# Causal attention in slots of four heads: maxima from row scores, exponentials from column scores, weighing on four array column strips

## The chip, the core and the metric

The kernel runs on one core of a Trainium2 chip, as one launch that computes everything. The metric is device microseconds from start to end; lower is better. TensorE (PE in the rows, PEld for its weight loads) multiplies matrices into the eight banks of PSUM; VectorE (DVE), ScalarE (ACT) and GpSimd (POOL) work elementwise; SyncE (SP) issues the DMAs. Each engine follows its own list of instructions in order, and they meet only through semaphores.

## The reference

The input is x of 8 sequences, 512 tokens, 128 channels. The output is x plus two branches of its layer-normalised tokens xn: a causal attention, which the change is about, and a stack of six layers of windowed attention and gated MLP, which it leaves alone.

```python
q_lat = (x @ Wq_down).reshape(b, t, H, L)             # H 16 heads, L 64; k and v alike
q_c, q_e = q_lat @ Wq_up_c, q_lat @ Wq_up_e           # 4 + 4 dimensions a head
q = concatenate([q_c, rope(q_e)]);  k alike;  v = v_lat @ Wv_up    # 8 dimensions a head
scores = einsum('bhqd,bhkd->bhqk', q, k) / sqrt(8)
scores = where(causal, scores, -inf)
att = softmax(scores, axis=-1)
y = einsum('bhqk,bhkd->bhqd', att, v)
return y @ Wc                                         # 128 x 128
```

Per sequence there are 16 heads of 512 x 512 scores under a causal mask, with only 8 dimensions to contract.

## The kernel before, in words

**Start.** The tokens of all 8 sequences are normalised and turned into `xT` (channels on partitions). The down and up weights are multiplied into five 128 x 128 matrices `wcomb`. This ends at about 36 us.

**The causal stage** runs over the batches b (sequences) and, in a batch, over 64 slots n, one for each head h and query tile qt of 128 queries. The helper `causal` (L254) runs a function `causal_slot` on each engine over the first batch, a hardware loop over the middle ones and the last batch with its drain; `earlier` (L263) gives the slot that lies a fixed lag behind. Within one turn of the slot the engines do, for different lags:

- GpSimd, `mask_q` (L1267): once a head it multiplies a stack of q by a 0/1 mask, so that of the four heads in a stack only one is left. The stack holds for four heads the terms hi·hi, hi·lo, lo·hi of q and k as rows (`stacks`, 128 rows), filled by SP with small transfers of 64 KB (`stack`, L292).
- TensorE (L402): the scores of 128 queries by (qt+1) x 128 keys as one fp32r product over all 128 rows into one of three banks, then the triangle `tri` added to the diagonal block by a bf16 product with the identity. The query rows lie on partitions. Seven slots later it transposes the divided exponentials, 128 x 128 blocks in fp32 (L416). Fifteen slots later it weighs the values: `v16` holds each head's values in 128 columns that are zero elsewhere, so that all heads add up into one bank `ps[4]` over the batch.
- VectorE (L997): the negated row maximum (L1013) and, five slots later, the division of the exponentials (L1009).
- ScalarE (L708): the exponential with the maximum as bias and the row sum as second output (L722), and the copy of the transposes to SBUF (L668, a helper that records every copy).

In the same lists stand the five projections of the next batch (`project_causal`, L384), their rotation and split into hi and lo on VectorE (`rope`, L972), the product with `wc` and the sum with x (L1019). Before the projections VectorE copies the batch's part of `xT` to `xb` (L970).

**After it** the weights of the first of six layers are loaded, once the last weighing product is done, and the rest of the kernel follows. L357 is the line of the helper that records every matrix product, so such rows are told apart by their tiles: `sb_xwin,sb_ptT` are the causal scores, `sb_tri,sb_identb` their masks, plain `sb_area` 128x512 and narrower the weighing. An fp32 product appears as two records, an fp32r or bf16 product as one; a transpose in fp32 is one.

In the windowed attention, unchanged, two kinds of products use halves of the array: scores with 64 stationary columns (`128*64 128x64`), whose two results go to partitions 0 to 63 and 64 to 127, and weighings with 64 rows (`64*128 64x256`), whose operands lie on partitions 0 to 63 and 64 to 127.

## Time and profile before

| | |
|---|---|
| time, median of 3 runs | 4157.45 us (4157.35 to 4159.3) |
| profiled execution: time, span | 4155.5 us, 4153.7 us |
| busy share TensorE, VectorE, ScalarE, GpSimd | 92%, 78%, 75%, 60% |
| mean granted TensorE clock | 0.971 |
| first causal score, last weighing product | 60.75 us, 709.9 us |
| DMA moved | 52.9 MB, 13 GB/s |

The span is the time from the first to the last instruction. Busy shares are means over the whole kernel; the causal stage is the first sixth of it. A row of the timeline gives the start, how long the group was busy, the engine, the line, the operation, the result and operands, the shape of weights and moving data, and the count; square brackets give idle time before it. Matrix products are pipelined: one product's time includes about 0.16 us in which the next already runs. The granted clock is a share of 2.4 GHz.

### The profile page before, as it was taken

The page shows a single profiled execution, that of the slowest core. Times are in us where ns is not written, and L with a number is a line of the kernel's source. Part 1 is how long each engine was busy: PE and PEld are TensorE (multiplying, and loading weights), DVE is VectorE, ACT ScalarE, POOL GpSimd, SP SyncE. Part 2 cuts the span into 40 slices and gives each one's busy share as a digit, 9 for nine tenths or more (in the row PEclk, how much of TensorE's full clock was granted, in tenths as well). Part 3 has the DMA queues.
Part 4 walks back from the last instruction along what each step waited for, and adds up shares of the span by engine and source line. Part 5 has one row for each costly group of instructions (what it writes and reads, how often), then busy time and mean ns, then how long its engine had stood idle before and what let it go on. Part 6 is the DMA issues. An engine that isn't in the chain of part 4 may idle for free.

```text
span 4153.7 us, 101302 instructions
## 1 busy us (share of the span) xinstructions
PE 3814.5 (92%) x30950; PEld 2939.8 (71%) x31328; DVE 3258.6 (78%) x5635; ACT 3109.2 (75%) x7150; POOL 2498.3 (60%) x2247
## 2 busy tenths in 40 slices
PE   6999998899998999988999989999889999899998
PEld 4666665677766777766777667777667776677776
DVE  5877876888867888768888678887688886788876
ACT  4777776788866888857888668887578886688875
POOL 1221221777745777737777457776377774577763
PEclk9999999999998999998999989999989999999999
DMA  2111111000010000010000100000100000000002
GB/s 79 42 32 31 29 39 35 2 0 0 0 28 1 1 0 0 1 28 1 0 0 0 28 1 1 0 0 1 28 1 0 0 0 28 1 1 0 0 1 68
DMA packets 53261, 52.86 MB, mean 13 GB/s; under 512 B 13574, under 2 KB 40452, under 8 KB 51972
## 3 DMA queue, kind: packets, MB, share of 16 engines
q1 hardware_dynamic: 52996, 49.77, 4.5%
q8 instruction: 113, 1.85, 0.2%
q14 instruction: 152, 1.25, 0.1%
HBM read 28.77 MB, written 4.19 MB: 8 GB/s over the span
## 4 chain that ended last, share of the span: by engine, by line
issue 26%; PE 24%; ACT 24%; DVE 21%; ACTq 2%; DVEq 2%; POOL 1%; SPq 0%; DMA 0%; POOLq 0%
PE bank L357 19%; ACT sb_area L668 12%; DVE sb_ssq L1105 10%; DVE sb_smax L1116 6%; ACT sb_area L777 5%; PE bank L416 3%; ACT sb_lnb L786 3%; ACT sb_lnb L789 3%; DVE sb_area L1093 1%; PE bank L503 1%; POOL sb_area L1336 1%; DVE sb_nmx L1013 1%; DVE sb_area L1119 0%; PE bank L532 0%; DVE sb_area L1009 0%
## 5 line engine op out<-in xcount | busy, mean ns | idle before, releaser
L668 ACT ACTIVATE sb_area<-bank 128x512 f32<-128x512 f32 (+4 forms) x3029 | 1570.3, 553 | 259.0 <-PE bank L357 182.3
L357 PE MATMUL bank<-sb_area 128*64 128x64 f32 (+4 forms) x16624 | 1286.1, 274 | 94.9 <-issue 57.8
L1093 DVE TENSOR_TENSOR sb_area<-bank,sb_rots 128x1024 f32<-128x1024 f32 x768 | 939.2, 1224 | 395.2 <-ACT sb_area L777 394.4
L1311 POOL TENSOR_TENSOR sb_area<-sb_area,sb_rn 128x512 f32<-128x512 f32 x768 | 784.8, 1043 | 608.5 <-ACT sb_rn L793 608.5
L1297 POOL TENSOR_TENSOR sb_area<-sb_area 128x512 f32<-128x512 f32 x768 | 967.9, 1278 | 78.3 <-DVE sb_area L1093 76.2
L357 PEld LDWEIGHTS bank<-sb_area 128*64 128x64 f32 (+2 forms) x16624 | 849.5, 151 | 200.6 <-issue 139.1
L357 PE MATMUL bank<-sb_wqk_hi,sb_xwin 128*128 128x512 f32 x1536 | 729.7, 477 | 53.9 <-DVE sb_xwin L1073 43.6
L357 PE MATMUL bank<-sb_area,sb_wvo 128*128 128x256 f32 x3072 | 728.3, 381 | 3.1 <-DVE sb_xT L1151 3.1
L357 PEld LDWEIGHTS bank<-sb_area,sb_wvo 128*128 128x128 f32 x3072 | 555.0, 190 | 78.3 <-issue 12.8
L503 PE MATMUL bank<-sb_ident,sb_area 128*128 128x128 f32 x3072 | 494.9, 285 | 33.4 <-ACT sb_area L668 31.0
L503 PEld LDWEIGHTS bank<-sb_ident,sb_area 128*128 128x128 f32 x3072 | 358.8, 144 | 227.6 <-issue 160.0
L1105 DVE TENSOR_REDUCE sb_ssq<-sb_area 128x8 f32<-128x512 f32 x768 | 486.7, 675 | 0.0
L777 ACT ACTIVATE sb_area<-bank 128x512 f32<-128x512 f32 x768 | 460.4, 600 | 30.9 <-PE bank L357 14.5
L1320 POOL TENSOR_TENSOR sb_area<-sb_area,sb_srec 128x512 f32<-128x512 f32 x384 | 400.3, 1042 | 88.4 <-DVE sb_srec L1131 88.4
L1270 POOL TENSOR_TENSOR sb_ptT<-sb_xwin,sb_hm 128x512 fp32r<-128x512 f32 x128 | 137.8, 1077 | 510.8 <-PE bank L357 494.1
L722 ACT ACTIVATE sb_area<-bank,sb_nmx 128x128 f32<-128x128 f32 (+3 forms) x512 | 270.1, 528 | 178.5 <-DVE sb_nmx L1013 175.6
L357 PEld LDWEIGHTS bank<-sb_wqk_hi,sb_xwin 128*128 128x128 f32 x1536 | 304.2, 198 | 111.3 <-issue 48.9
L1013 DVE TENSOR_REDUCE sb_nmx<-bank 128x1 f32<-128x128 f32 (+3 forms) x512 | 249.1, 487 | 125.4 <-PE bank L357 114.4
L357 PE MATMUL bank<-sb_wqk_lo,sb_xwin 128*128 128x512 f32 x768 | 315.4, 411 | 0.0
L820 ACT ACTIVATE sb_area<-sb_area 128x512 f32<-128x512 f32 x384 | 242.9, 633 | 76.4 <-DVE sb_area L1119 70.9
L357 PE MATMUL bank<-sb_xwin,sb_ptT 128*128 128x128 f32 (+3 forms) x512 | 286.9, 561 | 13.3 <-POOL sb_ptT L1270 8.4
L1129 DVE TENSOR_REDUCE sb_ssum<-sb_area 128x8 f32<-128x512 f32 x384 | 261.6, 681 | 45.2 <-ACT sb_area L820 40.0
(103 smaller groups left out, 4861.7 us busy)
## 6 DMA issues: line engine op xcount, KB each, us to landing
sb_xwin<-sb_p SPq DMA_DIRECT2D x256, 64.0 KB, 2.0
sb_area<-in_Wqkv SPq DMA_DIRECT2D x7, 1024.0 KB, 5.8
sb_area<-in_WvT SPq DMA_DIRECT2D x7, 512.0 KB, 7.3
sb_wo_bd<-in_Wo SPq DMA_DIRECT2D x14, 256.0 KB, 8.2
sb_area<-in_x SPq DMA_DIRECT2D x4, 512.0 KB, 5.7
sb_area<-in_x SPq DMA_DIRECT2D x8, 256.0 KB, 2.9
x_plus_causal<-sb_area SPq DMA_DIRECT2D x8, 256.0 KB, 2.3
out<-sb_area SPq DMA_DIRECT2D x8, 256.0 KB, 3.5
```

The source lines that it names most:

```text
L357: return nc.tensor.matmul(o, a, b, start=start, stop=stop, skip_group_check=True)
L503: m = nc.tensor.transpose(rbank[:, j * P:(j + 1) * P], qn[:, c, j * P:(j + 1) * P], ident[:, :])
L668: return nc.scalar.activation(o, i, ACT.Copy)
L722: nc.scalar.activation(ea(k // TT, qt, 0, (qt + 1) * P), ps[k % 3][:, 0:(qt + 1) * P], ACT.Exp, bias=nmx[:, k % 8:k % 8 + 1], accum_out=ls ...
L777: nc.scalar.activation(sqb[:, c % 2, :], pj[c % 2][:, :], ACT.Square).then_inc(S["sq"], 1)
L1013: nc.vector.tensor_reduce(nmx[:, k % 8:k % 8 + 1], ps[k % 3][:, 0:(k % TT + 1) * P], AX.X, ALU.max, negate=True).then_inc(S["c_max"], 1)
L1093: tt_(t12[:, c % 2, :, :].rearrange("p u (h d) -> p u h d", h=8), src, bc(rots[:, tt, s, :, :], [P, 2, 8, D], 2), ALU.mult).then_inc(S["ro ...
L1105: nc.vector.tensor_reduce(ssq[:, tt % 2, half, 8 * (c % 2):8 * (c % 2) + 8], sqb[:, c % 2, :].rearrange("p (h d) -> p h d", h=8), AX.X, AL ...
L1129: nc.vector.tensor_reduce(ssum[:, wp, :], d3, AX.X, ALU.add).then_inc(S["ssum"], 1)
L1297: pt_(qsum[:, c % 2, :].rearrange("p (h e d) -> p h e d", h=8, e=2), t12[:, c % 2, 0, :].rearrange("p (h e d) -> p h e d", h=8, e=2), swap ...
L1311: pt_(qn[:, c, :].rearrange("p (h d) -> p h d", h=8), qsum[:, c % 2, :].rearrange("p (h d) -> p h d", h=8), r, ALU.mult).then_inc(S["qn"], 1)
L1320: pt_(dd[:, wp, :].rearrange("p (h k) -> p h k", h=HP), dd[:, wp, :].rearrange("p (h k) -> p h k", h=HP), srec[:, wp, :].unsqueeze(2).to_b ...
```

## The change

The causal stage is rewritten; the rest stays. A slot is now a group of four heads of one batch, 32 slots in all, and all lists are written out over an iteration `it` from -2 to 7 and a head group `hg` of 0 to 3, without hardware loops.

- **Projections** of batch it+2 read `xT` itself and all go through bank 7, whose users take turns by one list (`m_order`, semaphore `m_free`): maxima, projections, values, output.
- **Stacks** hold each head on 32 partitions: 8 dimensions times four rows: three terms, and a fourth row that is 1 for k in two of the dimensions. q and k go to DRAM (`split_out`, six transfers of 256 KB) and come back in this order (`stack`, two transfers of 256 KB for each head group). Two batches are held.
- **Row scores** (`rows_of_scores`) for slot n1 = 4 it + 4 + hg serve only for the maxima: in eight units two heads at a time, each with 32 rows of the array, into banks 0 and 1, with the mask. VectorE takes both heads' maxima in one reduction (`maxima`). The maxima of a slot are turned once (`turn_max`), split in hi and lo, sent through DRAM and put into two of the stack's fourth rows of q (`max_rows`).
- **Column scores** (`columns_of_scores`) for slot n2 = 4 it + hg, four slots later: twelve tiles with the keys on partitions, 32 rows of the array each, in banks 2 to 4, with the mask. The product subtracts the maximum through the extra rows. ScalarE takes the exponential without bias or sum (`exp_columns`). No transposes.
- **Weighing** (`weigh_values`): four heads, each with 32 stationary columns, go to partitions 32r to 32r+31 of bank 5, and once more with `ones32` instead of the values for the sums, into bank 6. At a batch's end ScalarE takes exp(-ln(sum)), VectorE multiplies (`weighed_causal`, `divided`).
- GpSimd no longer masks anything.

```diff
+            def rows_of_scores(n, u):
+                a, hg, qt = n // 4, n % 4, u % 4
+                need(pe, "c_max", 8 * n + u)
+                if u == 0:
+                    pe.wait_ge(S[f"stack{hg}"], FULL * (a + 1))
+                keys = (qt + 1) * P
+                for x in range(2):
+                    r = 2 * (u // 4) + x
+                    rows = slice(32 * r, 32 * r + 32)
+                    mm(ps[x][:, 0:keys], stack_q[a % 2][rows, hg, qt * P:(qt + 1) * P], stack_k[a % 2][rows, hg, 0:keys],
+                       True, False)
+                for x in range(2):
+                    m = mm(ps[x][:, qt * P:keys], identb[:, :], tri[:, :], False, True)
+                m.then_inc(S["c_s1"], 1)
+
+            def columns_of_scores(n, j):
+                a, hg, r = n // 4, n % 4, j % 4
+                need(pe, "c_exp", 12 * n + j - 2)
+                if j == 0:
+                    pe.wait_ge(S[f"mrow{hg}"], 2 * 16 * (a + 1))
+                rows = slice(32 * r, 32 * r + 32)
+                o, k, q = ps[2 + j % 3], stack_k[a % 2][rows, hg, :], stack_q[a % 2][rows, hg, :]
+                for kt, c0 in (((0, 0),), ((1, 0),), ((2, 0), (3, 2 * P)))[j // 4]:
+                    mm(o[:, c0:c0 + T - kt * P], k[:, kt * P:(kt + 1) * P], q[:, kt * P:T], c0 == 0, False)
+                for c0 in (0, 2 * P)[0:1 + j // 8]:
+                    m = mm(o[:, c0:c0 + P], tri[:, :], identb[:, :], False, True)
+                m.then_inc(S["c_s2"], 1)
+
+            def weigh_values(n, kt, o, weights, last):
+                a, hg = n // 4, n % 4
+                e, c0 = ((et0, 0), (et1, 0), (et2, 0), (et2, 2 * P))[kt]
+                for r in range(4):
+                    m = mm(o[32 * r:32 * r + 32, kt * P:T], weights(kt, r), e[:, r, c0:c0 + T - kt * P],
+                           hg == 0 and kt == 0, hg == 3 and kt == 3)
+                if last:
+                    m.then_inc(S["c_pv"], 1)
...
+            for it in range(-2, B):
+                for hg in range(4):
+                    n2, n1 = 4 * it + hg, 4 * it + 4 + hg
...
+                    tiles(0, 1, 2)
+                    if n2 >= 1:
+                        end_of_slot(n2 - 1)
+                    if 0 <= n1 - 1 < SLOTS:
+                        turn_max(n1 - 1)
+                    unit(0)
+                    tiles(3)
+                    unit(1)
+                    tiles(4, 5)
+                    if hg < 2 and it + 2 < B:
+                        project_causal(it + 2, 2 * hg)
+                    if hg == 2 and it >= 1:
+                        causal_out(it - 1)
+                    unit(2)
+                    if n2 >= 0:
+                        weigh_causal(n2, 0)
+                    tiles(6)
+                    unit(3)
+                    if n2 >= 0:
+                        sum_causal(n2, 0, True)
+                    tiles(7, 8)
+                    if hg < 2 and it + 2 < B:
+                        project_causal(it + 2, 2 * hg + 1)
+                    if hg == 2 and 0 <= it + 1 < B:
+                        causal_values(it + 1)
+                    unit(4)
+                    if n2 >= 0:
+                        weigh_causal(n2, 1)
+                        sum_causal(n2, 1, True)
+                    tiles(9)
+                    unit(5)
+                    tiles(10)
+                    unit(6)
+                    tiles(11)
+                    unit(7)
+            end_of_slot(SLOTS - 1)
+            causal_out(B - 1)
...
+            def exp_columns(n, j):
+                T_, r = j // 4, j % 4
+                act.wait_ge(S["c_s2"], 12 * n + j + 1)
+                need(act, "c_pv", 3 * (n - 1) + T_ + 1)
+                w = T if T_ == 0 else T - P
+                nc.scalar.activation((et0, et1, et2)[T_][:, r, :], ps[2 + j % 3][:, 0:w], ACT.Exp).then_inc(S["c_exp"], 1)
...
+            def maxima(n, u):
+                r, qt = 2 * (u // 4), u % 4
+                dve.wait_ge(S["c_s1"], 8 * n + u + 1)
+                if u == 0 and n >= 2:
+                    dve.wait_ge(S["c_mt"], n - 1)
+                nc.vector.tensor_reduce(nmx[:, n % 2, 0:16].rearrange("p (r t) -> p r t", t=TT)[:, r:r + 2, qt],
+                                        banks[:, 0:2, 0:(qt + 1) * P], AX.X, ALU.max, negate=True).then_inc(S["c_max"], 1)
```

`end_of_slot` weighs and sums key tiles 2 and 3; `weigh_causal(n, kt)` and `sum_causal(n, kt)` call `weigh_values` with the values and with the ones; `tiles` and `unit` call the column and row scores where their slot exists.

## Rows read from the trace of the kernel before

**Rows 1.** The page, part 1: busy us (share of the span) and instructions of each engine.
```profile
PE 3814.5 (92%) x30950; PEld 2939.8 (71%) x31328; DVE 3258.6 (78%) x5635; ACT 3109.2 (75%) x7150; POOL 2498.3 (60%) x2247
```

**Rows 2.** Busy time by stretches: stretch, length, engines, granted clock, DMA share, GB/s; three batches.
```profile
138.00:219.00 81.00, 75.50 (x441) 50.75 (x440) 63.22 (x155) 59.50 (x193) 17.33 (x16) 0.98 0.13 34
...
300.00:382.30 82.30, 75.95 (x441) 51.07 (x441) 63.51 (x156) 59.77 (x194) 17.33 (x16) 0.98 0.13 33
...
628.00:710.00 82.00, 78.52 (x473) 54.08 (x473) 59.13 (x150) 62.76 (x202) 14.55 (x14) 1.00 0.05 13
```

**Rows 3.** Timeline of TensorE in the causal stage: start, us, engine, line, tiles, shapes, count.
```profile
694.09 0.48 PE L357 MATMUL bank<-sb_xwin,sb_ptT 128*128 128x512 f32 x1
...
697.69 0.61 PE L416 MATMUL bank<-sb_ident,sb_area 128*128 128x128 f32 x4
698.14 0.39 PE L357 MATMUL bank<-sb_area 128*128 128x128 f32 x2
698.28 0.48 PE L357 MATMUL bank<-sb_xwin,sb_ptT 128*128 128x512 f32 x1
698.60 0.23 PE L357 MATMUL bank<-sb_tri,sb_identb 128*128 128x128 bf16 x1
698.67 0.28 PE L416 MATMUL bank<-sb_ident,sb_area 128*128 128x128 f32 x1
698.79 1.02 PE L357 MATMUL bank<-sb_area 128*128 128x512 f32 x2
```

**Rows 4.** Timeline of TensorE in the windowed attention: full-array, column-half and row-half groups.
```profile
1004.22 1.89 PE L357 MATMUL bank<-sb_area,sb_wvo 128*128 128x256 f32 x8
...
1008.54 1.15 PE L357 MATMUL bank<-sb_area 128*64 128x64 f32 x32 [0.16 <-issue]
1009.62 0.44 PE L561 MATMUL bank<-sb_ident,sb_xs 128*128 128x128 f32 x2
1009.99 1.13 PE L357 MATMUL bank<-sb_area 64*128 64x256 f32 x8
1011.05 0.66 PE L503 MATMUL bank<-sb_ident,sb_area 128*128 128x128 f32 x4
```

**Rows 5.** Timeline of TensorE's weight loads there, with idle time before.
```profile
1009.99 0.73 PEld L357 LDWEIGHTS bank<-sb_area 64*128 64x128 f32 x8 [0.17 <-issue]
1011.05 0.42 PEld L503 LDWEIGHTS bank<-sb_ident,sb_area 128*128 128x128 f32 x4 [0.33 <-issue]
```

**Rows 6.** VectorE's reductions, six batches grouped by form (busy us, mean ns), and a start-up one.
```profile
L1013 DVE TENSOR_REDUCE sb_nmx<-bank 128x1 f32<-128x512 f32 x94 | 64.7, 689 | 12.7 <-PE bank L357 7.8
...
L1013 DVE TENSOR_REDUCE sb_nmx<-bank 128x1 f32<-128x256 f32 x95 | 40.1, 422 | 24.0 <-PE bank L357 24.0
...
4.52 1.22 DVE L957 TENSOR_REDUCE sb_lnm<-sb_area 128x8 f32<-128x1024 f32 x1 [0.75 <-DMA sb_area<-in_x]
```

**Rows 7.** ScalarE's exponentials of the causal stage by form, six batches.
```profile
L722 ACT ACTIVATE sb_area<-bank,sb_nmx 128x512 f32<-128x512 f32 x94 | 64.7, 689 | 32.8 <-DVE sb_nmx L1013 32.8
...
L722 ACT ACTIVATE sb_area<-bank,sb_nmx 128x384 f32<-128x384 f32 x94 | 54.6, 580 | 26.5 <-DVE sb_nmx L1013 25.8
```

**Rows 8.** Timeline before the first score.
```profile
35.52 7.65 DVE L970 COPY sb_area<-sb_xT 128x512 f32<-128x512 f32 x1 [9.39 <-ACT sb_xT L668]
...
43.31 3.75 PE L357 MATMUL bank<-sb_area 128*128 128x512 f32 x4 [8.46 <-DVE sb_area L970]
...
60.75 0.48 PE L357 MATMUL bank<-sb_xwin,sb_ptT 128*128 128x128 f32 x1 [8.43 <-POOL sb_ptT L1270]
```

**Rows 9.** TensorE by stretches: busy us, granted clock, DMA share, GB/s.
```profile
153.00:156.50 3.50, 1.10 (x10) 0.99 0.01 2
156.50:160.00 3.50, 3.45 (x9) 0.52 0.00 0
...
1308.00:1313.00 5.00, 1.89 (x8) 0.50 0.00 0
```

**Rows 10.** Timeline at the stage's end: last weighing products, and what waited for them.
```profile
705.17 4.70 PE L357 MATMUL bank<-sb_area 128*128 128x128 f32 x18
...
709.90 0.34 SPq L323 DMA_DIRECT2D sb_area<-in_Wqkv x1
...
719.42 2.19 ACT L668 ACTIVATE sb_wqk_hi<-sb_area 128x512 fp32r<-128x512 f32 x4 [8.91 <-DMA sb_qks<-in_qks]
```

398 lines of the change are left out of this document (208 added, 190 removed).

## The prediction

> **What bounds the kernel now.** I read the page's busy shares first [rows 1]: TensorE is the busiest engine, but that is a mean over stages. The table by stretches of time, cut at the batches of the causal attention, comes next [rows 2]. The stage runs from the first score at 60.75 us [rows 8] to the last weighing product at 709.9 us [rows 10], 649 us. In a batch of 81 to 82 us TensorE is busy 75 us, VectorE 63, ScalarE 60, GpSimd 17. TensorE bounds the stage, so a change gains what it takes off TensorE's stream of instructions and loses what it puts there. All that follows the stage has the same code and starts when the last weighing product is done; only the stage's end moves it.
>
> One head costs 4.19 us in the calm part of a batch (first score of one head at 694.09, of the next at 698.28). The timeline of such a head [rows 3] gives the prices at 2.4 GHz. An fp32 product is two records; the pair of 512 columns takes 1.02 us and one record 0.59, so a record of 512 columns costs 0.43 in the stream, of 128 columns 0.107. fp32r (scores) and bf16 (mask) columns cost half: 512 columns 0.213, 128 columns 0.053. A head has 1280 columns of scores (0.53), 512 of mask (0.21), ten transposes (1.07) and 1280 columns weighed in two records each (2.13), 3.95 us, with 0.04 for each mask's weights 4.1. Sixteen heads and 5.1 us of projections, values and output are 71 us; the other 10 to 11 us of a batch are waits around the projections.
>
> **Removed and added on TensorE.** I count by slot, the new unit: four heads, 32 slots; today one costs 20.4 us. Transposes (4.3 us) go. Weighing (8.5 us) becomes 16 products with 32 stationary columns each, on four column strips, and as many again for the sums. One after the other this would be 17.1 us, four abreast 4.27 us. Scores are computed twice: 5120 columns with 32 rows each for the maxima, and 5120 again as columns; masks 16 and 16.
>
> Do strips run abreast? [Rows 4] show halves. 32 records of 64 columns on two column halves take 1.15 us; one after the other they would be 32 x 0.053 + 0.17 = 1.9. Eight records of 256 columns on two row halves take 1.13; eight full-array ones take 1.89. So halves run in pairs, although each product is two records. Four abreast isn't shown. The ends are 4.27 us (four) and 8.5 us (two) a slot; I take four, since nothing in the pairs shows a shared limit. The Trainium skill, "TensorE: Matmul & The Clock Gate", Part 3, gives 2.38x for three column strips. If four strips were 3.2x by that, an estimate from that page, they would be 5.3 us and the kernel some 33 us longer than with my value; no run here shows it.
>
> What does changing the shape cost? In [rows 4] two full-array transposes start at 1009.62 and take 0.44, so the last starts 0.27 before their end, at 1009.79, and has its columns through at 1009.90. The row halves start at 1009.99: 0.09 later. Their group takes 1.13 where 4 x 0.216 + 0.16 = 1.02 is the columns and the tail: another 0.10, the first weights, which are not hidden. The loads agree: idle 0.17 before the halves and 0.33 before the return [rows 5], while in [rows 3] full-array groups follow each other without it. So a change of shape costs 0.09 plus the load: 0.107 for 128 fp32r columns, 0.03 for a 32-column strip, about 0.013 for bf16. The Trainium skill, "TensorEngine Tiling (Array Packing)", Key Properties, says that changing the mode, not just the tile, drains the engine, and lists 32-row tiles as a mode of their own; by it 32-row tiles pay what halves pay here, which the trace shows for halves alone.
>
> The new order changes shape all the time, since every 32-row score is followed by a full-array mask:
> - a tile of 512 columns: 0.20 + 0.213 + 0.10 + 0.053 = 0.57 us; 384 columns 0.52; 256+128 columns with two masks 0.59. Twelve tiles: 6.7 us.
> - a unit of row scores, two heads abreast, q+1 blocks of keys: 0.43 + 0.053(q+1). Eight units: 4.5 us.
> - weighing and sums: 4.27 + four changes at 0.12 + small gaps: 4.9 us; the turn of the maxima 0.1.
>
> 16.2 us a slot, some 6 of it shape changes. The bounds of a change of shape are 0 and 0.3 us (half clock); there are about 44 in a slot, so an error of 0.02 in each is 26 us of kernel time.
>
> **Waits added.** The row scores use one pair of banks, so unit u+1 is queued behind the reduction of unit u, and all of TensorE's later work behind it. VectorE takes 0.42, 0.69, about 0.96 and 1.22 us for 256 to 1024 columns ([rows 6], 1.06 ns a column, and 1.22 for 1024). Add 0.21 from the last mask column to its start and 0.06 back. A reduction of 1.22 us needs 1.5 us of other work behind its unit. Walking the written order, this holds for the first five units. Units 6 and 7 have only one tile each in between (0.52 to 0.59 us): 0.4 and 0.65 us of wait. A slot is 17.2 us. ScalarE's twelve exponentials are below 4 x 0.69 + 8 x 0.58 = 7.4 us [rows 7], the eight reductions 6.6: neither engine is near. In three slots of four two projections (0.85 each), or output and values, add 1.75: 18.95. A batch is 3 x 18.95 + 17.2 = 74, taken as 75 for small gaps that my count of a head misses too (4.1 against 4.19). GpSimd's masking and SP's 32 small transfers a batch are replaced by 8 transfers of 256 KB, 6 through DRAM before them, and the maxima's 3 per slot; these have one to four slots of lead, and I cost them at nothing. The cover for the maxima is three slots, 50 us, against four transfers of 2 to 3 us.
>
> **The pipeline's ends.** Today batches overlap without a seam. The new order has one pass of row scores only, seven with both, one of columns only.
> - First score: today 60.75 [rows 8]. The 7.65 us copy goes (7 us earlier), but one bank serves both projections (+2), and q and k go 1.5 MB out to DRAM and 0.5 back, about 12 us: 62 (56 to 68).
> - Row scores only: each unit is a bare chain of reduction and 0.61 + 0.053(q+1). A slot is 6.6 + 4.9 + 1.1 + 0.25 = 12.8; four are 51. TensorE is mostly idle there, as it was from 1308 to 1313 us (busy 1.89 of 5 us), where its clock was granted 0.50 [rows 9], the 1.2 GHz level. That adds up to 15; I take 8: 59.
> - Seven batches at 75: 525.
> - Columns only: 4 x 11.8 + 0.9 = 48. Last sums, behind the last exponential: 2.3.
>
> End at 62 + 59 + 525 + 48 + 2.3 = 696, against 709.9: 14 us earlier. The longer end (logarithm, exponential, product: +2.4 us) lies beside the weight load of 709.90 to 719.4 [rows 10] and costs nothing. With the clock held, the kernel takes 4157.45 - 14 = 4144.
>
> **The clock.** From 153 to 156.5 us TensorE is busy 1.10 of 3.5 us, and from 156.5 to 160 it is granted 0.52, although busy 3.45 [rows 9]. In the new slot the last tiles and units (about 13 to 17 us) stream for 1.1 of 3.4 us: the rest is changes of shape and waits on VectorE. I expect the lower level to come there in nearly every other slot and to last through the next slot's first tiles and sums, which take some 3 us more at half rate. That is 1.1 us a slot over 28: +31. Bounds: 0, and the whole stage at 1.2 GHz, where a slot is 27 to 32 us.
>
> **Forecast.** 4157.45 - 14 + 31 = 4175, say 4176. The profiled execution has a span of 4153.7 in a time of 4155.5, 2 us below the median, so differences carry over as they are.
>
> **Rivals.**
> 1. *The clock holds.* 4144 (4125 to 4160). For: a busy share over half in a slot as a whole. Against: [rows 9].
> 2. *Changing shape to 32-row tiles is cheaper than to halves.* Up to 44 x 0.09 = 4 us a slot, also no dip: 4060 to 4125. Against: the constant 0.09 in [rows 4, 5] both ways.
> 3. *Strips run only in pairs.* +4.27 x 32 = 137: 4280 to 4320. It would show as eight strip records taking four times one's stream time instead of twice.
> 4. *The clock stays low* (slower, and by much). A 32-row product may keep a quarter of the array at work; then the tiles and units of a slot hardly count as work and the level returns only sometimes. A slot at 26 to 27 us instead of 18.7: +230 to +250, 4380 to 4420. It decides once the granted clock of the seven full batches is under about 0.8.
> 5. *The extra work isn't the bound at all*, VectorE or DMA is: the first unit of each batch would wait on its stack. Each us there is 8 us; little speaks for it.
>
> **Chances.** Forecast (4150 to 4215) 0.35; clock holds 0.25; cheap changes 0.12; pairs only 0.08; clock low 0.17; the rest 0.03. A measurement of this kernel tells 0.2%, 8 us, from no change. Faster (under 4149): cheap changes 0.12 and most of clock holds 0.18, together 0.30. Same: 0.12. Slower: 0.58. The range takes in half of the cheap changes and half of the low clock: 4085 to 4410. The likeliest case alone is 4150 to 4215.
>
> **What would show it.** The score of a 32-row tile and its mask starting 0.09 after the columns of the one before are through; eight strip records of 512 columns in about 1.0 us; a full slot of 17 to 19 us at a clock of 1.00, with waits before units 6 and 7; the granted clock by stretches of 17 us between 60 and 700 us; first unit at 62 and last sum near 727. A slot under 15 us or over 24 at full clock would mean that my prices of the shapes are wrong.

## The result, and the profile after

The changed kernel takes 4292.9 us (median of 4 runs, 4288.9 to 4295.4) against 4157.4 us: 1.0324 times the time before, 95% interval 1.0306 to 1.0342. It is slower by 135 us, where 19 were forecast. The profiled execution has a span of 4287.1 us against 4153.7.

First the page of the changed kernel: span, busy shares, and the granted clock in 40 slices of 107 us.

```profile
span 4287.1 us, 98195 instructions
PE 4006.0 (93%) x32128; PEld 2850.4 (66%) x32128; DVE 3016.4 (70%) x4772; ACT 2853.0 (67%) x6048; POOL 2357.7 (55%) x2124
PEclk9878886699999899999999999999999999999999
```

TensorE is busier than in [rows 1], 4006 us against 3814, although it has hardly more products; VectorE, ScalarE and GpSimd all have less work than before. The clock row says where: it is below 9 in slices 2 to 8, which with the first are the causal stage, and like before behind it.

The first slice needs care, because there the granted clock and the durations disagree:

```profile
60.00:77.00 17.00, 11.66 (x39) 1.00 0.22 79
61.98 2.02 PE L382 MATMUL bank<-sb_xT,sb_area 128*128 128x512 f32 x2
```

The record says 1.00 from the first score to 149.5 us, but an fp32 product of 512 columns takes 2.02 us, where it takes 1.02 at 2.4 GHz in [rows 3], and such double durations last until about 146 us. In that stretch I go by the durations: the level was 1.2 GHz. From 150 us on the two agree in every row shown here.

The stage's two ends, from the timeline. The first row score starts at 59.96 us; SP's load for the layers, which waits for the last weighing product, is issued at 842.74, where it was at 709.90 in [rows 10].

```profile
59.96 0.47 PE L382 MATMUL bank<-sb_xwin 32*128 32x128 f32 x2 [12.59 <-DMA sb_xwin<-qk_rows]
842.74 0.35 SPq L348 DMA_DIRECT2D sb_area<-in_Wqkv  x1
```

842.74 - 709.90 = 132.8, and the spans differ by 133.4. So all of the loss lies in the stage. By stretches (us from the start, length, TensorE's busy time, granted clock, DMA share, GB/s), with the last row for the pass of column scores alone:

```profile
124.00:300.00 176.00, 171.35 (x952) 0.77 0.13 41
300.00:500.00 200.00, 194.04 (x1192) 0.79 0.16 50
500.00:700.00 200.00, 194.59 (x1198) 0.78 0.15 47
776.00:843.00 67.00, 64.80 (x425) 0.73 0.03 9
```

TensorE has work 97% of the time at a clock of 0.77 to 0.79 (the first row is too high by what was just said: with 22 us more at 1.2 GHz it is about 0.71); the three batches of [rows 2] were at 0.98 to 1.00. One calm batch slot by slot (a slot begins here with its first column mask), and a slot of the last full batch, which has no projections:

```profile
407.72:430.74 23.02, 22.36 (x135) 0.80 0.07 25
430.74:452.05 21.31, 20.65 (x134) 0.87 0.01 3
452.05:472.69 20.64, 19.98 (x147) 0.92 0.40 129
472.69:496.50 23.81, 23.15 (x131) 0.67 0.16 47
699.67:727.30 27.63, 27.52 (x130) 0.50 0.01 2
```

The same instructions take 21.3 us at 0.87 and 23.0 at 0.80. The slot at 0.50 takes 27.6 without projections, where the fourth, of the same form, takes 23.8 at 0.67. So the durations follow the clock. Read in steps of 0.1 us, the batch from 412.5 to 501.3 us has six dips to 0.50, together 34 us of 89: around 417.5, 433, 455, 475.5, 486 and 498 us. One long stretch at the full level and the longest dip:

```profile
437.00:453.00 16.00, 15.34 (x94) 1.00 0.01 2
480.50:490.50 10.00, 10.00 (x49) 0.51 0.36 107
```

The waits are small, 0.20 and 0.47 us before two of the eight units of a slot:

```profile
449.27 0.44 PE L382 MATMUL bank<-sb_xwin 32*128 32x384 f32 x2 [0.20 <-DVE sb_area L1115]
450.97 0.50 PE L382 MATMUL bank<-sb_xwin 32*128 32x512 f32 x2 [0.47 <-DVE sb_area L1115]
```

Where the clock is at 2.4 GHz the prices are the forecast ones. From the timeline of TensorE (`sb_xwin 32*128` and `sb_wqk_lo,sb_wqk_hi` are scores, `128*32` weighing on four strips):

```profile
541.54 0.50 PE L382 MATMUL bank<-sb_xwin 32*128 32x512 f32 x1
541.98 0.23 PE L382 MATMUL bank<-sb_identb,sb_tri 128*128 128x128 bf16 x1
542.13 2.79 PE L382 MATMUL bank<-sb_area 128*32 128x256 f32 x32
...
546.39 0.39 PE L382 MATMUL bank<-sb_wqk_lo,sb_wqk_hi 32*128 32x256 f32 x2
546.71 0.29 PE L382 MATMUL bank<-sb_tri,sb_identb 128*128 128x128 bf16 x2
546.92 0.44 PE L382 MATMUL bank<-sb_xwin 32*128 32x384 f32 x1
...
549.52 1.06 PE L382 MATMUL bank<-sb_area 128*32 128x512 f32 x8
550.51 0.44 PE L382 MATMUL bank<-sb_xwin 32*128 32x384 f32 x1
...
841.17 1.51 PE L382 MATMUL bank<-sb_area 128*32 128x256 f32 x32 [0.58 <-ACT sb_area L818]
```

A tile of 512 columns with its mask takes 542.13 - 541.54 = 0.59 us (forecast 0.57), a unit over two blocks of keys 546.92 - 546.39 = 0.53 (0.54), the eight strip records of 512 columns 550.51 - 549.52 = 0.99 ("about 1.0"). The 32 strip records that start at 542.13 already ran in a dip: 2.79 us, against 1.51 for the same at 841.17.

Setting each product of a dip to its time at 1.00 gives an estimate of the slots at full clock: 19.0 and 19.1 us for the slots at 430.74 and 452.05 (forecast 18.95), 17.2 for the one at 472.69 (forecast 17.2).

By passes, beside the forecast: row scores alone 63.4 us (59), seven full batches 123.77 to 776.17 = 652.4 (525, and 31 for the clock), columns alone with the last sums 66.6 (50), the start 1.6 us earlier than said (60.36, counted like the slots from the first mask; the first score itself is at 59.96). The question is therefore why the granted clock stays at three quarters in the full batches (0.76 by the record for all seven, 0.74 with the first stretch put right), and whether it alone is the loss.

### The profile page after: what moved, and what is told of

It is laid out like the page before. It is cut to its first block, busy times and chain, and to the rows that moved or that the text cites. A ratio compares the mean times of both kernels' runs of the same rounds, so it can differ in the third digit from the quotient of the medians.

```text
span 4287.1 us, 98195 instructions
## 1 busy us (share of the span) xinstructions
PE 4006.0 (93%) x32128; PEld 2850.4 (66%) x32128; DVE 3016.4 (70%) x4772; ACT 2853.0 (67%) x6048; POOL 2357.7 (55%) x2124
## 4 chain that ended last, share of the span: by engine, by line
PE 29%; issue 24%; ACT 22%; DVE 20%; ACTq 1%; DVEq 1%; POOL 1%; DMA 1%; SPq 0%; POOLq 0%
PE bank L382 27%; ACT sb_area L769 11%; DVE sb_ssq L1227 10%; DVE sb_smax L1238 5%; ACT sb_area L894 5%; ACT sb_lnb L903 3%; ACT sb_lnb L906 3%; DVE sb_area L1115 2%; PE bank L604 1%; DVE sb_area L1215 1%; POOL sb_area L1446 1%; DVE sb_area L1241 0%; PE bank L633 0%; ACT sb_rn L910 0%; ACTq L892 0%
## 5 line engine op out<-in xcount | busy, mean ns | idle before, releaser
L769 ACT ACTIVATE sb_area<-bank 128x512 f32<-128x512 f32 (+3 forms) x2517 | 1352.6, 578 | 251.8 <-PE bank L382 188.7
L382 PE MATMUL bank<-sb_area 128*64 128x64 f32 (+6 forms) x17520 | 1132.2, 304 | 7.4 <-DMA sb_area<-in_c_crot 2.8
L382 PEld LDWEIGHTS bank<-sb_area 128*64 128x64 f32 (+3 forms) x17520 | 743.7, 148 | 226.0 <-issue 177.3
L382 PEld LDWEIGHTS bank<-sb_area,sb_wvo 128*128 128x128 f32 x3072 | 555.0, 190 | 78.4 <-issue 12.8
L1115 DVE TENSOR_REDUCE sb_area<-bank 128x2 f32<-128x256 f32 (+3 forms) x256 | 211.5, 826 | 464.3 <-PE bank L382 464.1
L894 ACT ACTIVATE sb_area<-bank 128x512 f32<-128x512 f32 x768 | 460.6, 601 | 30.9 <-PE bank L382 13.9
L818 ACT ACTIVATE sb_area<-bank 128x384 f32<-128x384 f32 (+1 forms) x384 | 199.3, 523 | 416.6 <-PE bank L382 412.8
L1241 DVE TENSOR_TENSOR sb_area<-bank,sb_smax 128x512 f32<-128x512 f32 x384 | 265.6, 692 | 13.3
```

Of the source, the lines that this page charges most:

```text
L382: return nc.tensor.matmul(o, a, b, start=start, stop=stop, skip_group_check=True)
L769: return nc.scalar.activation(o, i, ACT.Copy)
L894: nc.scalar.activation(sqb[:, c % 2, :], pj[c % 2][:, :], ACT.Square).then_inc(S["sq"], 1)
L1115: nc.vector.tensor_reduce(nmx[:, n % 2, 0:16].rearrange("p (r t) -> p r t", t=TT)[:, r:r + 2, qt], banks[:, 0:2, 0:(qt + 1) * P], AX.X, AL ...
L1241: tt_(dd[:, wp, :].rearrange("p (h k) -> p h k", h=HP), s3, bc(smax[:, wp, :], [P, HP, 64], 2), ALU.subtract).then_inc(S["sub"], 1)
```

## The experiments

The theory on record with the runs: TensorE's stream has the length I worked out, and what is missing is the clock, lowered because products of 32 rows use little of the array or because changes of shape leave gaps. The rivals: the prices of that stream at full clock, or the waits, are wrong. Each kernel ran beside the kernel before on its chip (4154.5 to 4157.7 us).

### More columns in each tile: on the full array, or on 32 rows

```diff
+                mm(o, identb[:, :], lmask[:, 0, :], True, True)     # e1_fill_full
+                mm(o, k[:, 0:P], q[:, 0:T], True, True)             # e1_fill_rows
                 for kt, c0 in (((0, 0),), ((1, 0),), ((2, 0), (3, 2 * P)))[j // 4]:
```

> Work is added to the changed kernel (4292.9 us): ahead of the first score product of each of the 384 column tiles stands one more bf16 product over the whole array, 512 columns into the same bank, which the score product then overwrites. 0.213 us each at 2.4 GHz, 2.6 us a slot. Theory (the excess over my sum is TensorE's clock, which falls to 1.2 GHz where the array is lightly used): the level holds at 2.4 GHz in the full batches, where a slot takes about 21.2 us instead of the 23.3 of the changed kernel; in all about 4230 us, faster with more work. Rival (the slot is as long as it is for other reasons, waits or shape changes that I priced too low): the added work adds 12 x 0.23 us a slot, about 88 us: 4380.

Measured: 4386.3 us (4372.5 to 4400.1), ratio 1.0553 [1.0474, 1.0631]. That is the number of the rival without the clock, 4380. A slot of it without projections, at full clock, and 200 us in the middle:

```profile
793.69:813.33 19.64, 19.39 (x143) 1.00 0.01 3
300.00:500.00 200.00, 198.25 (x1115) 0.77 0.14 44
```

> The same added work in the stream, but with 32 rows of the array: ahead of the first score product of each column tile one more fp32r product of 512 columns on the same 32 rows, overwritten by the real one. 0.213 us each at 2.4 GHz as in the twin with full-array products. Theory (a 32-row product leaves most of the array idle and does not keep the clock up): the granted clock stays as low as in the changed kernel or lower, and the added work costs its columns at a mixed clock, 3 to 3.5 us a slot: about 4400. Rival (any stream of products keeps the clock up): the same as the twin, 4230. Rival without the clock: 4380, with an unchanged granted clock.

Measured: 4490.5 and 4571.6 us, too far apart for a ratio with an interval; the mean clock over the whole kernel was 0.905 and 0.882, in the twin 0.926 and 0.920. The profile is of the longer execution, its full slots 30.2 to 34.3 us long. The same 200 us of it:

```profile
300.00:500.00 200.00, 199.36 (x889) 0.55 0.13 40
```

The slot at 1.00 is worth most: 19.64 us, less 12 products at 0.213 (2.56), is 17.1 us, and the forecast for this slot was 17.2. Against the rival (waits or changes of shape priced too low) it is this slot that speaks, not the time. The size of the first result is a miss: twelve more full-array products in a slot did not lift the clock (0.71 to 0.84 from 124 to 900 us), they cost their own time and some more. But the two kernels have as many columns and as many changes of shape, and differ by 90 us at the least (4490.5 against 4400.1): in the profiled executions 512 columns more on 32 rows brought the level down to 0.55, the same columns on 128 rows left it at 0.77. The added products also differ in type, fp32r and bf16; the trains below are all of bf16.

### Column scores over all 128 rows

```diff
-                o, k, q = ps[2 + j % 3], stack_k[a % 2][rows, hg, :], stack_q[a % 2][rows, hg, :]
+                o, k, q = ps[2 + j % 3], stack_k[a % 2][:, hg, :], stack_q[a % 2][:, hg, :]
```

> The column scores are taken over all 128 rows of the stacks instead of the 32 rows of one head, so that a tile holds the sum over four heads of score minus maximum (the output is not the reference's). Same columns, same masks, no change of the array's shape inside a tile. By my prices a tile falls from 0.57, 0.52, 0.59 us to about 0.31, 0.26, 0.31: 3.2 us less a slot at a full clock, less about 1 us of new waits on the maxima. Theory with the clock: the level rises too, a slot goes from 23.3 to about 17 us, columns-only slots from 16 to 9: about 4090 (4070 to 4140). Rival without the clock: 32 x 3.2 = 100 us less, 4190.

Measured: 4110.1 us (4109.8 to 4110.3), ratio 0.9888 [0.9859, 0.9917]. The separation of the heads is left out: each column score sums the four heads of a stack.

```profile
300.00:500.00 200.00, 185.07 (x1525) 0.95 0.21 66
```

The time lies in the range of the theory with the clock (4070 to 4140) and well under its rival's 4190: with the same columns the clock is 0.95 and the kernel 183 us faster than the changed one. The edit takes away both suspects at once, though, the 32 rows and the change of shape.

### Dense blocks spread over the slot

```diff
                     if n2 >= 1:
-                        end_of_slot(n2 - 1)
+                        weigh_causal(n2 - 1, 2)
+                        sum_causal(n2 - 1, 2, False)
...
                     tiles(3)
+                    if n2 >= 1:
+                        weigh_causal(n2 - 1, 3)
+                        sum_causal(n2 - 1, 3, True)
                     unit(1)
...
                     if n2 >= 0:
-                        weigh_causal(n2, 1)
-                        sum_causal(n2, 1, True)
                     tiles(9)
+                    weigh_causal(n2, 1)
                     unit(5)
                     tiles(10)
+                    sum_causal(n2, 1, True)
```

> Same instructions in another order on TensorE: the weighing and the sums, full-array work in blocks of 1.3 us, are cut in two and spread: key tile 2 stays after the first three tiles of the next slot, key tile 3 goes behind the fourth tile, the weighing of key tile 1 stands after tile 9 and its sums after tile 10, in front of row units 5 and 6. Five changes of shape more a slot (about 0.5 us), waits for the maxima of units 6 and 7 smaller (0.5 us). Theory (clock): no lightly used stretch is left, the level holds at 2.4 GHz, a slot takes 19 us instead of 23.3, the whole 4292.9 - 28 x 4.2 = 4175 (4160 to 4230 if the level still falls at times). Rival without the clock: the waits alone, -15 to +15: 4275 to 4310.

Measured: 4424.5 us (4403.2 to 4445.8), ratio 1.0645 [1.0523, 1.0766], and against both expectations. I had thought that the weighing, the stream's dense part, would hold the level if it came at shorter distances. The level was at 0.50 most of the time instead (0.56, 0.63, 0.55 in the three stretches from 124 to 700 us), and the shorter blocks seldom raised it. The edit also has five more changes of shape in a slot, so order and changes aren't parted here. One slot of it happened to be at full clock, and confirms the price of the stream once more (a slot with output and values; forecast 18.95):

```profile
728.59:747.67 19.08, 18.62 (x147) 1.00 0.43 140
```

### The pass of row scores alone, kept at work

```diff
+                if it == -1:
+                    fill(30)      # full-array bf16 products of 512 columns into ps[2]
...
                             rows_of_scores(n1, u)
+                            if n2 < 0:
+                                fill((1, 2, 3, 3)[u % 4])
```

> The changed kernel with TensorE kept at work in the pass of row scores alone: 30 full-array bf16 products of 512 columns (nothing reads them) ahead of that pass, where TensorE is idle anyway, and one to three more behind each unit, where it waits for VectorE. Theory (the clock is the mis-sized term; it is at 1.2 GHz in that pass because TensorE works too little there): the granted clock of the four slots is 1.00, a slot takes 12.8 to 13 us as forecast, where it took 16.8, 16.8, 15.85 and 14, so the first full slot starts some 12 us earlier (112 instead of 123.8 us); with nothing else changed in the seven full batches the kernel takes about 4280. Rival (the prices of that pass, not the clock, are what I got wrong): the slots stay at 16 us or grow by the 4 us of products added to each, 4293 to 4310.

Measured: 4286.9 us (4284.9 to 4288.9), ratio 1.0318 [1.0288, 1.0348]; by the ratio that is not told apart from the changed kernel's 1.0324. What the run shows stands in its trace. Two slots of that pass, and the first full one:

```profile
74.62:87.84 13.22, 10.47 (x56) 1.00 0.02 4
87.84:100.69 12.85, 9.91 (x61) 1.00 0.51 166
...
112.50:133.36 20.86, 20.20 (x103) 0.81 0.10 28
```

Each slot has 18 x 0.213 = 3.8 us of products more and is shorter all the same: 13.2 and 12.85 us, where the same slots took 16.80 and 15.85. The forecast for full clock was 12.8. The first full slot starts 11.3 us earlier, as expected. And it starts at 2.4 GHz, falls 3 us later, at 115.5 us, is back at 122 and falls again at 132 (0.81 in all): so the order of the full slot brings the level down by itself, it is not left over from the pass before. Of the 11 us the profiled execution keeps 4 (spans 4283.1 and 4287.1); slots further on fell to a lower share, 0.65 against 0.78 from 500 to 700 us.

### Scores of a group first, then its masks

Units and tiles are put into groups, most of one unit and one or two tiles: first all products with 32 rows, then all masks. The work is the same, the changes of shape fall from some 44 to 26 in a slot, and scores of different row strips stand next to each other; in three of the groups unit and tiles share a strip. The list of a slot, abridged, with remarks of mine:

```diff
+                    group((), (0, 1))
+                    ...                      # weighing and sums of key tile 2, turn_max
+                    group((0,), (2,))
+                    ...                      # key tile 3
+                    group((1,), (3,))        # project / output
+                    group((2,), (4, 5))      # key tile 0
+                    group((3,), (6, 7))      # its sums, project / values
+                    group((4,), (8,))
+                    group((5,), (9, 10))     # key tile 1
+                    group((6,), (11,))       # its sums
+                    group((7,), ())
```

> The same work in another order: a unit of row scores and one or two tiles of column scores together, first all their 32-row products, then all their masks, so that a full slot changes the array's shape some 26 times instead of 44, and products of different row strips stand next to each other. By my prices a full slot takes 15.5 to 16 us at 2.4 GHz instead of 18.95 or 17.2, and a batch 62 to 64. Theory (the missing time is the clock's, and it is low because changes of shape and 32-row products leave the array's use low): time comes off the stream in any case, and the clock rises as well, since the same columns lie closer together: 4045 if it is held, 4150 to 4200 if it stays at about 0.8. Rival (changes of shape cost little and the 32-row columns alone lower the clock): 4240 to 4290.

Measured: 4039.9 us (4038.2 to 4041.6), ratio 0.9723 [0.9695, 0.9752]: faster than both kernels. Its batch, slot by slot, and one group on the timeline:

```profile
373.40:388.30 14.90, 14.33 (x136) 1.00 0.12 39
388.30:403.28 14.98, 14.40 (x136) 1.00 0.02 5
403.28:419.11 15.83, 14.46 (x147) 1.00 0.48 143
419.11:433.10 13.99, 12.48 (x131) 1.00 0.34 107
```

```profile
405.99 0.38 PE L382 MATMUL bank<-sb_wqk_lo,sb_wqk_hi 32*128 32x256 f32 x2
405.99 0.50 PE L382 MATMUL bank<-sb_xwin 32*128 32x512 f32 x1
406.42 0.28 PE L382 MATMUL bank<-sb_tri,sb_identb 128*128 128x128 bf16 x2
406.54 0.22 PE L382 MATMUL bank<-sb_identb,sb_tri 128*128 128x128 bf16 x1
406.60 1.11 PE L382 MATMUL bank<-sb_area 128*128 128x128 f32 x8
```

Unit and tile start at the same time (405.99) and run abreast; together they take 0.61 us until the next product, where apart they were 0.53 + 0.59. The clock is 0.99 between 300 and 500 us. The estimate with the level held was 4045, but its parts were not right to that measure: a batch takes 59.7 us, where 62 to 64 were expected, and the 2 to 4 us a batch went to dips elsewhere (0.91 from 124 to 300 us) and to the pass of row scores at 1.2 GHz. That the sum hits is partly luck; that the clock rose is not, it reads 0.99 where the changed kernel has 0.79.

To part the order of blocks from the grouping, the next kernel keeps that order but has each score's masks right behind it (in outline):

```diff
                 for u in us:
                     ...                                       # two row scores
+                    ...                                       # their two masks
                 for j in js:
                     ...                                       # column scores
+                    ...                                       # their masks
-                for u in us: ...                              # masks
-                for j in js: ...                              # masks
```

> The order of blocks of the merged kernel (weighing, sums, units and tiles in the same places), but each score product has its masks right behind it again, so that a slot changes the array's shape some 44 times as in the changed kernel. By the prices at 2.4 GHz this is 80 to 90 us over the 32 slots: 4125 if the level is held. Theory (the changes of shape leave gaps, and with 32-row products between them the clock falls): the granted clock of the full batches is under 0.75 and the kernel takes 4300 to 4430. Rival (the places of the dense full-array blocks are what holds the level in the merged kernel): clock over 0.93 and 4120 to 4150.

Measured: 4352.0 us (4337.0 to 4367.0), ratio 1.0468 [1.0431, 1.0506]. Three slots in a row of it:

```profile
318.62:350.21 31.59, 31.59 (x134) 0.50 0.06 18
350.21:377.49 27.28, 27.28 (x134) 0.62 0.01 2
377.49:396.17 18.68, 18.68 (x146) 1.00 0.44 143
```

So it is the grouping. The pair also separates the stream from the clock: the third slot's place in a batch costs 18.68 us here at full clock and 15.83 there. These 2.85 us are the grouping as a whole: fewer changes of shape and columns that now run abreast, less 1.4 us of idle time that the shorter slot has (15.83, busy 14.46). Over 28 slots that is 80 us of the 312 between the kernels; the rest goes with the level, 0.65 against 0.99 from 300 to 500 us.

### 32-row products added to the groups

```diff
+                    mm(o, k[:, 0:P], q[:, 0:T], True, True)
                     for kt, c0 in (((0, 0),), ((1, 0),), ((2, 0), (3, 2 * P)))[j // 4]:
```

> The merged kernel with one more 32-row product of 512 columns ahead of each tile's scores, on the tile's own strip (nothing reads it): 12 x 0.213 = 2.6 us a slot, 82 us in all, without one more change of shape. Theory part A (a 32-row product holds the level less than a full-array one): the clock of the full batches falls under 0.85 and the kernel takes 4250 to 4450. Rival (only the gaps count, and this adds none): the clock stays at 0.95 or more and the kernel takes 4120 to 4135.

Measured: 4103.6 us (4103.3 to 4104.0), ratio 0.9871 [0.9852, 0.9890], clock 0.97 between 300 and 500 us. Part A of the theory misses here: the level held. (The time is 64 us more and not 82, since in the groups with two tiles the added products run abreast: 8 x 0.213 = 1.7 us a slot; one went from 14.98 to 16.71.) One product of 32 rows more in a group is not enough to bring the level down; it stands abreast with others in most groups, so it isn't the stream on one strip that the theory was about. The two suspects had to be measured by themselves.

### Trains of one form

Ahead of the pass of row scores alone of the merged kernel, products that nothing reads, of bf16, one form at a time. The two kernels differ in the trains alone; each was run once, and only its clock and durations are read.

```diff
+            def trains():                # first kernel
+                strip(60, (0,))          # 32 rows x 512 columns on row strip 0
+                full(70)                 # 128 rows x 512 columns
+                strip(80, (0,))
+                full(40)
+                strip(160, (0, 1, 2))    # three strips in turn, a bank each
+                full(40)
+                mixed(60)                # 32 x 512, then full 128: two changes of shape
+                full(60)
+            def trains():                # second kernel
+                strip(120, (0, 1, 2))
+                full(60)
+                strip(140, (0, 1))
+                full(60)
+                pairs(50, T)             # full 512, then 32 x 64: two changes of shape
+                full(60)
+                pairs(60, P)             # full 128, then 32 x 64
+                full(60)
```

> The merged kernel with trains of products that nothing reads put ahead of the pass of row scores alone, to read the granted clock of each form by itself. All have 512 columns of bf16: 60 with 32 rows on one row strip, 70 on the full array, 80 on one strip, 40 full, 160 on three strips in turn, 40 full, 60 pairs of one with 32 rows and a full one of 128 columns, each pair with two changes of shape, 60 full. That is 130 to 170 us more in all. In the kernel that added 32-row products to every tile of the merged order the level held; in the one that added them to the order with a mask behind each score it sank to 0.55. Theory A (a 32-row product holds the level as any other; only gaps lower it): one strip at 1.00 in the middle, pairs below 1.00. Theory B (a 32-row product on one strip counts for less of the array): the level falls within the train on one strip, and the first such train doesn't raise it, while three strips abreast, at 0.07 to 0.11 us a product, keep it; the pairs fall as well.

The trains of the first kernel by stretches, cut so that none holds a change of the level: one strip; full; one strip; three strips; pairs.

```profile
46.20:71.90 25.70, 25.70 (x61) 0.50 0.43 143
76.00:88.90 12.90, 12.90 (x61) 1.00 0.00 1
93.00:119.50 26.50, 26.50 (x63) 0.50 0.00 0
130.20:141.90 11.70, 11.70 (x161) 1.00 0.01 1
155.00:190.00 35.00, 35.00 (x94) 0.50 0.00 0
```

Theory B. One strip streams for 26.5 us without a gap (0.42 us a product) at 1.2 GHz; the first such train never rose, the second fell from the 2.4 GHz that the full products had reached. Three strips abreast stay at 1.00, at 0.073 us a product. The last row has the form of the changed kernel's tile in bf16, 512 columns on 32 rows and a full-array mask: it fell from 1.00 at 154 us, and then a pair takes 0.75 us at 0.50, and it stays there.

> A second set of trains before the merged stage, bf16 again: 120 products of 32 rows and 512 columns on three strips in turn, 60 full ones of 512 columns, 140 on two strips in turn, 60 full, 50 pairs of a full product of 512 columns and one of 32 rows and 64 columns (two changes of shape in each pair, nearly all the work on the full array), 60 full, 60 such pairs with full products of 128 columns, 60 full. The first set showed one strip without a gap at 1.2 GHz and three abreast at 2.4. If the share of the array alone decides, pairs with 512 full columns stay at 1.00 although a third of their time lies in changes of shape, and the pairs with 128 columns fall because of what they stream in all; two strips abreast, half the array, are the open case between. If changes of shape lower the level by themselves, both kinds of pair fall. The train on three strips, begun at the low level, shows whether strips abreast can also raise it: by share it rises. Price of a pair at 2.4 GHz by my changes of shape: 0.213 + 0.027 + 0.2 to 0.25 = 0.45 to 0.5 us, and 0.3 us with 128 columns.

The second kernel: two strips; pairs of 512 full columns; pairs of 128 full columns.

```profile
68.80:83.90 15.10, 15.10 (x140) 1.00 0.01 1
96.90:119.50 22.60, 22.60 (x101) 1.00 0.00 0
137.00:154.00 17.00, 17.00 (x91) 0.50 0.00 1
```

Two strips abreast hold 1.00. So do the pairs of 512 full columns: 22.6 us for 50.5 pairs, 0.45 each (as estimated), of which 0.24 are columns and 0.21 the two changes of shape. Only where little is left between the changes, 0.08 us of columns in a pair that takes 0.29 at full clock, does the level fall. The train on three strips, begun at 1.2 GHz, rose. Changes of shape that take 0.21 of every 0.45 us are thus no sufficient cause; 32 rows on one strip are, and both together, in the form of the changed kernel's tiles, are what its slots mostly consist of. Which of the two does more in them, the trains don't say. The Trainium skill, "TensorE: Matmul & The Clock Gate", in its part on the second failure mode, tells of oscillation where TensorE idles briefly and often between groups; the pairs of 128 columns fit that, the pairs of 512 columns held 1.00 with gaps as long, and the strip at 0.50 had no gap at all.

### The ends of the merged kernel

Two kernels add the burst and the products behind the units of the first pass to the merged order, the second with more of them (two to five) and one ahead of each group in the pass of columns alone.

> The merged order together with the products that keep TensorE at work in the pass of row scores alone (30 ahead of it, one to three behind each unit). Theory: as for the merged order, less 10 to 15 us for that pass, and the first full slot begins at 2.4 GHz: about 4030 if the level is then held through the full batches, 4135 to 4190 if it falls in them again. Rival: no shorter than the merged order alone.

Measured: 4031.6 us (4025.2 and 4037.9), ratio 0.9703 [0.9667, 0.9740]. The profiled execution (the longer one) was 7 us ahead of the merged kernel's at the first full slot and 16 us at the last, and gave all of it back in the last pass, where the level sank to 0.50 (17.34 us for a slot that takes 10.2 at 1.00 in the merged kernel):

```profile
549.82:567.16 17.34, 17.34 (x98) 0.50 0.00 1
```

> The merged kernel with products that keep TensorE at work at both ends of the stage: 30 full-array ones of 512 columns ahead of the pass of row scores alone, two to five behind each of its units, and in the pass of column scores alone one ahead of each group. Theory: the pass of row scores alone takes four slots of 13 us at clock 1.00 (in the kernel that had one to three behind a unit, two of them were at 0.78 and took 15.3 and 13.0), the pass of columns alone four of 11 to 12.5 us instead of 15.5, 17.3 and 12.7: 4018 to 4030, against 4154 to 4157 of before, a ratio of 0.967 to 0.970. Rival (the level at the ends hangs on something that these products don't reach): no shorter than 4032.

Measured: 4031.3 us (4028.5 to 4034.5), ratio 0.9697 [0.9683, 0.9711]. In the first pass the expectation holds (three slots of four at 1.00, 13.9, 13.3 and 12.3 us), and the last pass stays at 1.00:

```profile
543.92:556.30 12.38, 12.38 (x106) 1.00 0.01 1
```

But the products added there take what they bring, about 1.5 to 2 us a slot. It ends 1 us above the range expected, next to the rival's 4032, and from the kernel with fewer added products (4031.6) it isn't told apart. The merged order alone is 2.8% faster than the kernel before, with the ends kept at work 3.0%; the 9 us between them are at the edge of what the intervals tell.

## Why the prediction was right in sign and wrong in size

**The clock, the step that failed.** I costed it at 31 us in the full batches and 8 in the first pass. Measured, the full batches take 652.4 us. At full clock they would take about 514, an estimate from the slots of 19.0 to 19.1 and 17.2 us above: six batches of 74.4, a seventh of 70.7, because it has no projections (I counted seven alike at 75), less 2.5 for what the first batch hasn't yet to weigh and put out. So the clock costs 138 us in them, where my sum has 31. It costs 12 instead of 8 in the first pass, and up to 16 in the last, where I had nothing. 107 + 4.4 + 16.3, less 10.5 for the batches and 1.6 at the start, is 115.6 us; the stage's end was missed by 115.4 (842.7 against 727.3), the time by 117.

The reason is what I took for work. I read [rows 9], where the level fell behind a stretch with little on TensorE, as a matter of the time in which columns stream, and counted the columns of a 32-row product like those of a full one; hence a dip only near the units that wait, and a return soon behind it. That dip exists: in the calm batch two of the six, around 433 and 498 us, lie across a slot's end, in every other slot as forecast, 14 us at 1.2 GHz. The other four, 20 us, lie behind the first tiles and in the middle of slots, where my sum had the full level. The train on one strip shows what was missing: products of 32 rows without any gap ran at 0.50. The level came back behind blocks of weighing (at 456, 477, 491 and 501 us), though not behind each: the sums at 480.4 and 484.0 us ran at 1.2 GHz.

**Rival 4 had the mechanism**, a quarter of the array at work, as far as the train on one strip shows it (the part that the changes of shape have beside it stays open), and its sign, "decides once the clock is under about 0.8"; measured was 0.76, with a time between the forecast and the rival's 4380 to 4420, since the dense blocks do bring the level back in most slots. I gave it 0.17 for want of any row with a 32-row product. Such a row was missing, but the sign to look for was there: a new form of instruction fills half the slot, and nothing in the trace of before says how the clock takes it. It should have had the larger part of the chance.

**Prices of shapes: right.** 0.59 against 0.57 for a tile, 0.53 against 0.54 for a unit, a slot 19.0 to 19.1 against 18.95 and 17.1 to 17.2 against 17.2, a slot of the first pass 12.85 against 12.8. The sum of the 0.09 us and the exposed load, measured on halves in [rows 4, 5], holds for 32 rows. Rival 2 (cheap changes) falls. The bound of 0.3 us for a change at half clock was too high, though: in the bf16 pairs of 128 columns the two changes take 0.21 us at either level (0.29 - 0.08 and 0.37 - 0.16), and in the fp32r tile 0.32 at 2.4 GHz (0.59 - 0.27) and 0.41 at 1.2 (0.94 - 0.53, between the column masks at 430.74 and 431.68). In keeping with that a slot at 0.50 took 27.6 us, 1.6 times 17.2 and not twice.

**Four strips abreast: right.** 0.99 us for eight records that would take 3.4 one after another. Rival 3 falls. The Trainium skill, "TensorE: Matmul & The Clock Gate", Part 3, has 2.38x for three column strips; here it is 3.4 with the change of shape, so my estimate of 3.2 from that page was the worse one.

**Waits: right in place, somewhat long.** 0.20 and 0.47 us before units 6 and 7 (forecast 0.4 and 0.65); VectorE and ScalarE are busy 264 and 221 us of the stage's 783. Rival 5 falls.

**Start, end and DMA: right.** First score 59.96 (62, bounds 56 to 68); the longer end hides beside the weight load, as the difference of the spans (133.4) and of the stage's ends (132.8) shows.

**With the clock held** the forecast was 14 us faster (4144). No run showed the changed order with the level held throughout, since its own slots bring it down. Worked out, it is 4293 - 138 - 12 - 16 = 4127, 17 below my sum, mostly by the batches (11) and by the clock of the first pass (8), which stands in the 4144 too. So the change does take work off TensorE's time, as the sum said, and the clock takes it back five times over.

## What to carry to other kernels

Count what TensorE does by the share of the array it keeps at work, not by its busy time: a stream of 32-row products on one strip showed 100% busy and ran at half clock, and the same products on two or three strips abreast ran at full. Where products on strips must alternate with full-array ones, put all the strips' products of a group together and the full ones behind them; here that saved 2.85 us of a slot at full clock and, with the level, 253 us of the changed kernel. Hold the granted clock against the duration of one known product before you build on it; in two of these traces it read 1.00 over 80 us and more (60 to 146 us in the changed kernel, 60 to 173 in the one with the order alone) in which products took twice their time. Where a change brings a form of instruction that no row of the trace has, a short train of that form alone in the existing kernel, read by its granted clock, costs one run.

## What the runs showed of the hardware

- The granted clock depends on the form: 0.50 for one row strip streamed without a gap over 26 us, 1.00 for two or three strips abreast and for the full array. How the chip weighs rows against gaps stays open: pairs with 0.21 us of change of shape in 0.45 us held 1.00, pairs with 0.21 in 0.29 didn't.
- The order of the same products counts. Spreading the dense blocks over the slot, with five changes of shape more, took 0.79 down to 0.63 (300 to 500 us) and the time up by 132 us; full-array products in every tile changed the level little (0.77).
- A change of shape scales little with the clock: two of them take 0.21 us in a bf16 pair at 1.2 and at 2.4 GHz, 0.41 and 0.32 in an fp32r tile.
- Products on different row strips start within 0.01 us of each other and share the time fully: 0.073 us each on three strips, 0.108 on two, 0.213 on the full array.
- Kernels whose level wavers also vary from run to run (4490 to 4572, 4403 to 4446, 4337 to 4367), the merged one at 0.99 hardly (4038 to 4042). Times between the low ones were therefore compared only where they differ by more than that.
